# Block sums of unscaled integers, added to x on VectorE, in a fused Flamingo block

## The reference, cut to what matters

```python
def quant_dequant_act_1x128(x):              # one scale per row and block of 128 columns
    amax = jnp.max(jnp.abs(xb), axis=-1, keepdims=True)
    safe = jnp.maximum(amax, ACT_EPS)
    q = (xb * (FP8_MAX / safe)).astype(jnp.float8_e4m3fn)
    return (q.astype(jnp.float32) * (safe / FP8_MAX)).reshape(E, M, K)
# the same for ctx, with one scale per block of 128 rows x 128 columns
return jnp.einsum('emk,enk->emn', xq, wq)

x = x + jnp.tanh(g_xattn[0]) * _L0_xattn_ref(_layernorm(x), ctx_2048)
x = x + jnp.tanh(g_ffn[0]) * _L0_ffn_ref(_layernorm(x), Wa, Wp, w_std, w_rec)
```

## Time and profile before

| | |
|---|---|
| median of 3 runs | 578.65 us |
| the profiled execution | 577.93 us, of it 576.2 us from the first to the last instruction (the span) |
| prologue, up to the first transpose of maxima | 98.0 us |
| bodies b = 0, 1, 2 | 130.9, 132.9, 122.6 us |
| body b = 3 | 91.8 us |
| busy: TensorE, VectorE, ScalarE, GpSimd | 84%, 60%, 46%, 34% of the span |
| mean granted TensorE clock | 0.953 of 2.4 GHz |

### The profile page before, as it was taken

The page is one execution under the profiler, slowest core; times in us unless marked ns, Lnnn a source line. Parts: engine busy times, 40 slices in busy tenths (PEclk is TensorE's granted clock), DMA queues, the critical chain, the costliest instruction groups (busy, mean ns, idle before and its releaser), DMA issues.

```text
span 576.2 us, 8459 instructions
## 1 busy us (share of the span) xinstructions
PE 482.2 (84%) x2408; PEld 346.9 (60%) x2408; DVE 343.2 (60%) x970; ACT 262.6 (46%) x575; POOL 193.2 (34%) x288
## 2 busy tenths in 40 slices
PE   0036887887998999898798999898798999999977
PEld 0024765555776768665575768665576667666646
DVE  4779647579675353479776235568866116546522
ACT  0856333666544322556554322446565423434540
POOL 4665829137322252126422243124622100212210
PEclk9999999998897999798898999898899899999999
DMA  7202064332400243332400144422300134234001
GB/s 248 117 1 73 4 193 97 97 89 67 118 1 2 61 101 116 120 82 51 132 0 1 41 100 114 128 61 60 84 0 1 28 88 101 66 88 110 20 18 74
DMA packets 28022, 42.55 MB, mean 74 GB/s; under 512 B 8272, under 2 KB 8528, under 8 KB 27984
## 3 DMA queue, kind: packets, MB, share of 16 engines
q1 hardware_dynamic: 26448, 41.97, 26.2%
q10 hardware_dynamic: 1536, 0.14, 0.2%
...
## 4 chain that ended last, share of the span: by engine, by line
PE 57%; DVE 20%; ACT 11%; issue 6%; DMA 2%; ACTq 1%; SPq 1%; POOL 1%; DVEq 0%; POOLq 0%
PE pv_bank L631 10%; PE mm_bank L509 10%; PE mm_bank L510 9%; PE mm_bank L511 9%; ACT work L883 4%; DVE max_bank L1103 4%; PE max_bank L600 4%; PE exp_bank L617 3%; PE mm_bank L661 3%; PE mm_bank L659 3%; PE mm_bank L660 3%; PE turn_bank L517 2%; ACT tile_buf L822 2%; DVE x_amax L1056 2%; DMA col_root<-in_L_ffn_w_rec 1%
## 5 line engine op out<-in xcount | busy, mean ns | idle before, releaser
L1103 DVE CUSTOM_DVE_ANT_0 max_bank<-max_bank,causal 128x512 f32<-128x512 f32 (+3 forms) x256 | 119.1, 516 | 37.3 <-PE max_bank L600 34.5
L406 POOL TENSOR_SCALAR_AFFINE_SELECT work<-work 128x384 f32<-128x384 f32 x64 | 34.2, 534 | 270.0 <-ACT work L883 270.0
L883 ACT ACTIVATE work<-exp_bank 128x512 f32<-128x512 f32 (+1 forms) x192 | 91.1, 523 | 3.2 <-PE exp_bank L617 2.7
L617 PE MATMUL exp_bank<-q_stack,k_stack 97*128 97x512 f32 (+3 forms) x256 | 73.8, 371 | 7.8 <-ACT work L883 4.9
L631 PE MATMUL pv_bank<-work,v_aug 128*33 128x256 f32 (+3 forms) x512 | 75.1, 435 | 0.0
L600 PE MATMUL max_bank<-k_stack,q_stack 96*128 96x512 f32 (+3 forms) x256 | 65.1, 351 | 10.4 <-DVE row_max L1103 8.8
L1086 DVE SCALAR_TENSOR_TENSOR qk_lo<-mm_bank,col_root,qk_hi 128x512 fp32r<-128x512 f32 x32 | 24.0, 750 | 75.6 <-ACT qk_hi L856 75.6
L856 ACT ACTIVATE qk_hi<-mm_bank,col_root 128x512 fp32r<-128x512 f32 x32 | 22.0, 688 | 84.1 <-PE mm_bank L511 84.1
L617 PEld LDWEIGHTS exp_bank<-q_stack,k_stack 97*128 97x128 f32 x256 | 44.7, 197 | 25.2 <-ACT work L883 15.8
L600 PEld LDWEIGHTS max_bank<-k_stack,q_stack 96*128 96x128 f32 x256 | 46.6, 200 | 21.9 <-DVE row_max L1103 12.0
L509 PE MATMUL mm_bank<-xt_hi,w_hi 128*128 128x512 f32 x128 | 57.3, 448 | 2.3 <-DVE xt_lo L1139 1.6
...
## 6 DMA issues: line engine op xcount, KB each, us to landing
q_stack<-qk_hi SPq DMA_DIRECT2D x128, 64.0 KB, 2.0
k_stack<-qk_hi SPq DMA_DIRECT2D x128, 64.0 KB, 2.0
x_all<-in_x SPq DMA_DIRECT2D x16, 256.0 KB, 3.9
ctx_raw<-in_ctx SPq DMA_DIRECT2D x16, 256.0 KB, 4.1
...
out<-x_all SPq DMA_DIRECT2D x16, 256.0 KB, 2.1
...
```

The costliest lines, as they stand in the source:

```text
L406: pool.affine_select(out=three, in_=three, compare_op=ALU.is_ge, fill=0.0, base=0, pattern=[[0, 3], [1, P]], channel_multiplier=-1)
L617: last = pe.matmul(bank[:, col:col + T - P * i], k_stack[0:97, s, j, P * i:P * i + P], q_stack[0:97, s, j, P * i:T], start=True, stop=True)
L883: act.activation(prob[j][:, UNIT_COL[k]:UNIT_COL[k] + UNIT_LEN[k]], exp_bank[(3 * j + k) % 2][:, 0:UNIT_LEN[k]], ACT.Exp, scale=SCALE).the ...
L1103: last = dve.tensor_tensor_reduce(max_bank[unit % 2][:, col:col + width], max_bank[unit % 2][:, col:col + width], causal[:, T - width:T], ...
```

## The change

The integers are no longer scaled back before they are transposed. `scale_down` and `first_down` are gone. A value of at most 4 significant bits needs no low part, so `turned_lo` stays for the layernormed H tiles alone, ctx's integers lie in `wt_hi` and x's integers in `wt_lo`. The product of row tile i and block k is one matmul into a bank of its own (`partial_sum`), without accumulation over k: 16 matmuls of 512 columns a batch where there were 48. Each bank holds four sub-blocks t of 128 columns with their own ctx scale; VectorE adds them one by one to x with a scale per row, `coef` = x's scale times ctx's scale times the gate (`coefficients`, one small instruction per tile): 64 instructions of 128x128 a batch (`add_sum`) where there were 4 of 128x512. In the loop a sum goes to `mm_bank[k % 2]`, and TensorE waits for VectorE to have added the sum two before it. The cross product of a tile now comes in two halves, S0 to S7, of two blocks each. In `FILL` the statistics, layernorm, scales and rounding of x lie two to four gaps earlier, S0 comes in step 3, S7 in step 5, and H3 one gap later, behind A0. In the prologue tanh of the gates no longer comes ahead of the first layernorm on ScalarE, four banks take the sums, and x tiles 0 and 1 are rounded on VectorE, 2 and 3 on GpSimd.

```diff
 FILL = [
-    ["Q2", "W0", "W1", ""],
-    ["K2", "W2", "W3", ""],
+    ["Q2", "W0", "W1", "W2"],
+    ["K2", "W3", "", ""],
     ["Q3", "", "", ""],
-    ["K3", "", "X0", "X1"],
-    ["S0", "X2", "X3", "S1"],
-    ["S2", "H0", "H1", "S3"],
-    ["", "H2", "H3", "A0"],
-    ["q0", "A1", "k0", "q1 k1"],
+    ["K3", "X0", "S0 X1", "S1 X2"],
+    ["S2", "S3", "X3", "S4"],
+    ["S5", "", "S6 H0", "S7 H1"],
+    ["", "", "H2", "A0 H3"],
+    ["A1 q0", "k0", "", "q1 k1"],
 ]
-LN1 = {(2, 0): [0], (2, 1): [1], (2, 2): [2], (2, 3): [3]}
-LN2 = {(5, 0): [0, 1], (6, 0): [2, 3]}
+LN1 = {(1, 0): [0], (1, 1): [1], (1, 2): [2], (1, 3): [3]}
+LN2 = {(5, 1): [0, 1], (6, 1): [2, 3]}
...
+            def partial_sum(n, i, k, first=False):
+                at = NK * i + k
+                if first:
+                    if i:
+                        pe.wait_ge(s_summed, at - NK + 1)
+                elif at < 2:
+                    pe.wait_ge(s_qklo, 8 * n - 1 + k)
+                else:
+                    pe.wait_ge(s_summed, 16 * n + at - 1)
+                pe.matmul(sum_bank(first, i, k)[:], wt_lo[:, k, P * i:P * i + P], wt_hi[:, k, 0:C],
+                          start=True, stop=True).then_inc(s_cross, 1)
...
                 elif kind == "S":
-                    split_product(mm_bank[i % 2][:], rows_of(xt_hi, i), rows_of(xt_lo, i),
-                                  cols_of(wt_hi, 0, C), cols_of(wt_lo, 0, C), s_cross)
+                    pe.wait_ge(s_thi, 12 * n + NT + i // 2 + 1)
+                    for k in (2, 3) if i % 2 else (0, 1):
+                        partial_sum(n, i // 2, k)
...
-            def scale_down(n, k):
-                act.wait_ge(s_round, 8 * n + k + 1)
-                for j in range(NK):
-                    last = act.activation(part, part, ACT.Copy, scale=down)
...
-            def residual(n, i):
-                dve.wait_ge(s_cross, NT * n + i + 1)
-                chain(dve.scalar_tensor_tensor(x_tile(n, i), like_x(mm_bank[i % 2][:], n), gates[:, 0:1],
-                                               x_tile(n, i), ALU.mult, ALU.add), wait_apart)
+            def add_sum(n, i, k, first=False):
+                at = NK * i + k
+                wait_apart(dve, s_cross, 16 * n + at + 1)
+                if k == 0:
+                    wait_apart(dve, s_coef, NT * n + i + 1)
+                else:
+                    wait_apart(dve, s_sum, 48 * n + 3 * at)
+                for t in range(NT):
+                    if k and t == NT - 1:
+                        wait_apart(dve, s_summed, 16 * n + at)
+                    x_part = x_tile(n, i)[..., P * t:P * t + P]
+                    last = dve.scalar_tensor_tensor(x_part, like_x(sum_bank(first, i, k)[:, P * t:P * t + P], n),
+                                                    coef[:, i, t, k:k + 1], x_part, ALU.mult, ALU.add)
+                    last.then_inc(s_sum if t < NT - 1 else s_summed, 1)
...
+            def add_half(n, half):
+                i = half // 2
+                for k in (2, 3) if half % 2 else (0, 1):
+                    add_sum(n, i, k)
+                if half % 2:
+                    x1_stat(n, i)
...
-            own = {(1, 0): [(x_stat, 0), (x_stat, 1)],
-                   (1, 1): [(x_stat, 2)],
-                   (1, 2): [(x_stat, 3)],
-                   (2, 1): [(x_scales, 0)],
-                   (2, 2): [(x_scales, 1)],
-                   (2, 3): [(x_scales, 2), (rounding, 4)],
-                   (3, 0): [(x_scales, 3), (rounding, 5)],
-                   (3, 1): [(rounding, 6)],
-                   (3, 2): [(rounding, 7)]}
+            own = {(0, 2): [(x_stat, 0), (x_stat, 1)],
+                   (0, 3): [(x_stat, 2), (x_stat, 3)],
+                   (1, 2): [(x_scales, 0)],
+                   (1, 3): [(x_scales, 1)],
+                   (2, 0): [(x_scales, 2)],
+                   (2, 1): [(x_scales, 3), (rounding, 4)],
+                   (2, 2): [(rounding, 5)],
+                   (2, 3): [(rounding, 6)],
+                   (3, 0): [(rounding, 7)]}
```

312 lines of the change are left out of this document (158 added, 154 removed).

## The result

The changed kernel takes 585.5 us (median of 4 runs, 585.19 to 590.68) against 579.0 us; the ratio is 1.013, with a 95% interval from 1.007 to 1.019. Measured again, beside the experiments, it was 586.3 against 578.6 us, ratio 1.014 (1.010 to 1.019). It is slower, and the forecast of 570.1 us with a range from 556 to 584 was wrong in its sign.

What follows compares the result with a forecast made beforehand. TensorE was taken to bound step 4 and the tail, with VectorE busy 14.9 of 15.5 us in step 3. Three bodies at -2.0 and the prologue's -2.5 gave -8.5 us: 570.1 us, own range 559 to 577, with rivals 556 to 584.

Steps and rivals of the forecast that it cites:

- price of an addition: VectorE's 128x128 additions: 0.28 us each from start to start, duration near 0.37 us; 17.9 us a batch.
- step 2: Loop body, two x scales and three masks added to VectorE: ends at 11.2 us, +0.3 us.
- ScalarE's moved work: ScalarE ends no step by its sum; priced at nothing but the latency taken out of the chain of X.
- the clock: TensorE's clock falls in the loop: 0.9 us a body given back, leaving -2.0 of -2.9 us.
- first rival: VectorE's additions cost over 0.31 us each: slower, 583 us at 0.33, 593 us at 0.37; chance 0.2.
- Step 1: Loop body, one turn and the statistics between maxima go: -1.3 us, still bound by K2 at half clock.
- Step 0: Loop body, W2 and four statistics come, mostly covered by VectorE's idle time: +0.4 us.
- third rival: TensorE's clock stays low another 12 us in steps 3 to 6 of each body: 579 us; chance 0.12.
- Step 3: Loop body, K3, X0 to X2, S0 and S1: 12.0 us without the 2.68 us low-part wait, -3.5 us.
- Step 6 and the tail: End of a body: VectorE late and A0, H3 waiting, +1.4 us; A1 and q0 waiting for H3, +1.2 us.
- Prologue: Before the loop: earlier first layernorm and additions, last low part at 71.5 us instead of 73.8; -2.5 us.
- second rival: VectorE keeps out of the way, steps 3 to 5 take only what TensorE needs: 554 us; chance 0.13.

Runs made afterwards that it cites:

- e10: e9 with ScalarE's layernorms of x moved out from between step 1's exponentials and two VectorE scales moved ahead of Q3; 552.4 us, ratio 0.953.
- e2: Changed kernel with the fourth x block's scales and a rounding moved behind the third pair of maxima in step 2; 577.6 us, ratio 0.997.
- e8: e2 with each matmul of the ctx blocks issued three times, same sums; 571.3 us, ratio 0.984.
- e6: e2 with a row tile's four matmuls accumulated in one bank and added once over 512 columns, leaving out the separate block scales; 541.8 us, ratio 0.935.
- e14: Changed kernel with H2 and H3 turned into the two matmul banks, H3 ahead of A0 and q0 ahead of A1; 572.5 us, ratio 0.989.
- e11: e10 with the matmuls of the ctx blocks issued once, as in the changed kernel; 555.0 us, ratio 0.958.
- e3: Kernel before the change, x and ctx products cut to their high parts, VectorE's loop low parts of x and ctx left out; 554.4 us, ratio 0.957.
- e9: e8 with H2 and H3 turned into the two matmul banks, H3 ahead of A0 and q0 ahead of A1; 564.6 us, ratio 0.960.
- e7: e2 with one addition of 512 columns for each matmul instead of four of 128, leaving out their ctx scales; 558.0 us, ratio 0.963.

## Why the prediction was wrong

The forecast was 8.5 us less; the spans say 7.4 us more. The price of an addition was right. What failed: a stall of 3.2 us in step 2, a step that had been put at +0.3; ScalarE's moved work, which had been priced at nothing; and the clock, 5.4 us in body 1 by the split where 0.9 had been put.

Step by step for body b = 1, forecast and measured (windows above less):

| step | 0 | 1 | 2 | 3 | 4 | 5 | 6 | 7 and tail | sum |
|---|---|---|---|---|---|---|---|---|---|
| forecast | +0.4 | -1.3 | +0.3 | -3.5 | -2.0 | +0.6 | +1.4 | +1.2 | -2.9 |
| measured | -1.6 | -1.3 | +3.6 | -1.1 | -2.1 | +2.6 | +1.3 | +2.0 | +3.5 |

- **The price of an addition** was right: eight in 2.16 us are a start distance of 0.26 us at a duration of 0.34, against 0.28 and 0.37 forecast. The first rival (over 0.31 us each) is out. The Trainium skill, "VectorE: DVE Perf Modes", "The DRAIN you can't avoid", says that the next operation waits for an empty pipe, and that one which isn't held starts earlier; these additions start 0.26 us apart with 0.34 us each.
- **Step 2 failed** (+0.3 forecast). "It ends at 6.7 + 2.8 + the scales between its maxima = 11.2" leaves 1.7 us for what stands between them. It was 3.0 us, from 262.93 to 265.93, with a rounding and the new coefficients in it, and the third pair of maxima is queued behind it: TensorE stands 3.2 us, in each of three bodies. I had priced these instructions one by one, and not asked which of them stand ahead of a release. At the full clock and without them the step is 10.3 us (e10). e2 prices the stall at 8.7 of the 16.2 us between forecast and the second measurement; in body 1 it takes 2.4 us out of step 2. The other 1.8 us, from 12.1 to 10.3, go only with e10, which moves layernorms behind step 1's exponentials and two scales ahead of Q3.
- **ScalarE, priced "at nothing", failed.** Its sum did stay small (8.66 us of 11.48 in step 1), but its order counted: its exponentials stand behind the moved layernorms, TensorE waits 1.19 and 0.99 us for them, and Q3 behind these runs at half clock. Step 1 "came out" at -1.3 by luck: the forecast had it "bound by K2 at half clock as before", but K2 ran at the full clock (0.23 us a matmul), and the step took 11.48 to 11.49 us in all three bodies. In body b = 0, where the clock was 1.00 before too, it grew, from 11.1 us. In e10 it takes 9.6.
- **Step 0** came out 2.0 us under its forecast, at a clock of 1.00 where it was 0.85 (3.1 us of half clock gone, which is 1.6 us by the split); nothing in the forecast says so, and in body b = 0 it is only 0.4 us shorter than before, at 0.82 against 1.00.
- **The clock failed.** "Of this I give back 0.9 for the clock": body 1 has 30.9 us of half clock where it had 20.1, 5.4 us of length in the split above (bodies 0 and 2: 8.5 and 1.9). Step 5 is 2.0 us over its forecast at a clock of 0.76; in e8, at 1.00, it is 12.8 us long with 2.8 us of added matmuls in it. The third rival had the mechanism, with 12 us more of half clock a body against 10.8 measured, but a chance of 0.12 and 579 us, since I took much of it to lie under VectorE's cover. The rival also had the place only in part: by the windows steps 3 to 6 gained 8.5 us of half clock and step 2 gained 6.9, while steps 0 and 1 lost as much. How much lies under VectorE's cover differs by step: from e2 to e8 step 4 goes from 0.89 to 1.00 and stays at 11.7 and 11.9 us, step 5 goes from 0.76 to 1.00 and falls from 15.0 to 12.8 us with 2.8 us more matmuls. And the rival's "step 6, the emptiest" was misread: step 3 has 80% busy time in the earlier trace rows, step 6 has 82%.
- **Step 3** failed by 2.4 us ("I take 12.0"). K3 behind the stall starts its matmuls at 0.43 us, and X2's turn stands behind S1's matmuls, which need the banks that S0's additions still read; S0 was over at 12.7 us of the step, not at 11.2:

```profile
280.20 0.50 PE L562 MATMUL mm_bank<-wt_hi,wt_lo 128*128 128x512 f32 x1 [0.94 <-DVE x_all L1095]
281.24 0.50 PE L562 MATMUL mm_bank<-wt_hi,wt_lo 128*128 128x512 f32 x1 [0.53 <-DVE x_all L1095]
281.57 0.66 PE L523 MATMUL turn_bank<-ident,tile_buf 128*128 128x128 f32 x4
```

  The clock is not the whole of it: e2 has 0.97 in this step, with VectorE busy 14.3 us of 14.8. With one addition a block (e6) it is 12.6 us.
- **Step 4** came out as forecast, with TensorE waiting for additions.
- **Step 6 and the tail** came out at +1.3 and +2.0 against +1.4 and +1.2, for the reasons given, though q0 in the tail also runs at 0.43 us a matmul; that they could be had at less than nothing, 14 us below the changed kernel (e14), I had not seen.
- **Prologue:** first layernorm at 11.7, first addition at 42.8, last statistics at 66.0 us were all within 1.2 us of the forecast (12.2, 44, 66). But q0 started at 72.7, not 71.5, and the first transpose at 96.8, not 95.5: the first product of V, whose matmuls start 0.43 us apart at first, ends at 64.9, and ScalarE copies V before the last two layernorms. (The column of the granted clock shows 1.00 for this stretch; the distances of the matmuls say otherwise. Before, V's first product at 65.7 us ran at 0.23 us a matmul.) The events, in order, are ScalarE's and TensorE's:

```profile
64.88 0.60 ACT L909 ACTIVATE v_aug<-exp_bank 128x512 f32<-128x512 f32 x1 [4.50 <-PE exp_bank L517]
```

```profile
60.40 0.77 PE L515 MATMUL exp_bank<-w_hi,xt_hi 128*128 128x512 f32 x1 [0.65 <-DVE xt_lo L1175]
60.96 0.63 PE L516 MATMUL exp_bank<-w_lo,xt_hi 128*128 128x512 f32 x1
61.39 0.63 PE L517 MATMUL exp_bank<-w_hi,xt_lo 128*128 128x512 f32 x1
...
72.70 0.50 PE L515 MATMUL mm_bank<-xt_hi,w_hi 128*128 128x512 f32 x1 [1.41 <-DVE xt_lo L1175]
```

- **The second rival** (VectorE out of the way, 554 us) had a size that the kernel can reach: e11 is at 555 us with all of VectorE's small additions (e3, at 554, has none of them). What stood against it in the changed kernel was in large part where VectorE's load, and ScalarE's, stood: 31 us lie between it and e11.

Of the loss against the kernel before, then: taking away is worth 24.5 us (e3); the stall costs 8.7 (e2) and the order of turns 14 (e14), both with the clock that they cost; the layernorms' place costs some 4 more (e10 against e9, with the scales moved too). What the additions cost can't be added to these, since e6 and e7 were made from e2. Nor are the single gains sure to add up: no run has the edits of e2 and e14 together and nothing else.
